# A gelu MLP with per-row experts in fp32r: block 1's first layer computed plainly, weight sums transposed on VectorE, x of block 0 loaded in two halves

## Chip, cores and metric

The kernel runs on one core of a Trainium2 chip. The metric is the device time of one execution in microseconds. One execution was also recorded by the hardware profiler; all rows shown here are from it.

## What is computed

```python
h = jax.nn.gelu(jnp.einsum('bnd,hd->bnh', x, fc1_w) + fc1_b, approximate=False)
shared = jnp.einsum('bnh,sh->bns', h, fc2_w) + fc2_b
We = experts_w[indices]
be = experts_b[indices]
expert_x = jnp.einsum('bnh,bph->bnp', h, We) + be[:, None, :]
x = x + jnp.concatenate([shared, expert_x], axis=-1)
```

x is 32 x 256 x 256, fc1_w 1024 x 256, fc2_w 192 x 1024; each of the 32 rows of the batch picks one of 16 experts of 64 x 1024. Everything is float32.

## The kernel before

Work goes in 16 blocks (n = 0 to 15) of two batch rows, so 512 tokens (4 tiles of 128). Each float32 operand is split in two fp32r parts, a high one (a copy, made by ScalarE) and a low one (the difference, made by VectorE or GpSimd), and each product is three matmuls: high by high, high by low, low by high. The engines run five hand-written instruction streams that meet only through semaphores, each in its written order.

**First layer (fc1).** Block 0 is computed plainly: `conv_chunk(j)` (j = 0 to 7) makes 128 hidden features for all 512 tokens with 6 matmuls of 512 columns, into one of four PSUM banks `fc1_ps`; ScalarE turns it into gelu, two chunks make a pair. Blocks 1 to 15 use a seven-product scheme on half-size matrices (`product`, L875): per block two groups, per group seven products of 6 matmuls of 256 columns, so 84 matmuls. It needs four sums of weight pieces (W_S1 to W_S4), made once, and four sums of x pieces per block (X_T1 to X_T4: `x_sum`, `x_sums_high`, `x_sums_lo`), and VectorE's adds (`add_c11`, `add_v`, `add_c12`, `add_c22`).

**Hidden features.** ScalarE's `pair_high` writes a pair's high part to `ht`, GpSimd's `pair_lo` (L303) the low part. ScalarE's `gelu_free` keeps it from overwriting a `gelu` buffer (there are two) until the low part of the pair that lay in it is done.

**Second layer (fc2).** `fc2_units(n, r, first, count)` multiplies pair r by the weights, 3 matmuls of 256 columns a unit (L911, L913, L915), 96 in all for a block. It runs one block behind fc1, its units put between the products. It writes `acc_ps`, one bank per batch row, which VectorE's `drain(n, b)` (L728) adds to `resid`. Before the first unit of block n on a bank TensorE waits for `drained` of block n - 1 on it:

```python
if r == 0 and n >= 1 and u in (0, T * 2):
    pe.wait_ge(drained, R * (n - 1) + b + 1)
```

**Start.** TensorE transposes block 0's x (`x0_bank`) and the fc1 weights (`w1_bank`), the latter by halves; between them it runs 20 and 10 small matmuls (`warm`) that compute nothing. The transposed weight sums also come from TensorE (`s_bank`, 16 transposes of 128x128 into `acc_ps`, from what GpSimd's `weight_sum` made of the rows of fc1_w). fc2_w, the experts and x of the later blocks come to `pieces` in 32-row pieces and are transposed by VectorE (`w2_square`, `experts_square`, `x_square`), through the two PSUM banks `tr_ps`. SyncE issues most loads (`load_x`, `load_w1`, `load_experts`, `load_x_pieces`), ScalarE's queue the first half of fc1_w, fc1_b and the expert numbers `index`. GpSimd's `residual(n)` (L295) adds the biases to `resid`.

In the trace's rows `fc_ps` is `fc1_ps`, and `work` holds fc1_w's rows and later scratch.

Of the kernel before, what the change touches and what calls it, by code (L numbers as in the profile page):

```python
# [15 lines left out]
def cond_mlp_residual(nc, x, index, fc1_w, fc1_b, fc2_w, fc2_b, experts_w, experts_b, out):  # L16
# [24 lines left out]
    X_B11, X_B21, X_B22, X_T1, X_T2, X_T3, X_T4 = range(7)  # L41
    BANK_A, BANK_B, BANK_C = (0, 1), 2, 3
# [12 lines left out]
    w1_v = fc1_w.rearrange("(q k c) d -> q c k d", q=Q, c=S)  # L55
    w2_v = fc2_w.rearrange("(a r) (q j) -> q r a j", r=S, q=Q)

    ctx = ExitStack()
    with ctx:
# [34 lines left out]
        s_in = work[:, 2048:4096].rearrange("p (s m c) -> p s m c", s=4, m=4)  # L94
# [18 lines left out]
        w1_loaded = [sem(f"w1_loaded{n}") for n in range(2)]  # L113
        w2_loaded = sem("w2_loaded")
# [11 lines left out]
        s_tr = sem("s_tr")  # L126
# [11 lines left out]
        x0_hi = sem("x0_hi")  # L138
        w1_hi = sem("w1_hi")
# [37 lines left out]
        def group(n, g):  # L177

            return GROUPS * (n - 1) + g

# [18 lines left out]
        def _(sp):  # L199
# [35 lines left out]
            load_x(0)  # L235
            load_w1(sp, 1)
            for q in range(Q):
# [8 lines left out]
                .then_inc(b2_loaded, 16)  # L246
            load_x(1)
# [41 lines left out]
        def _(pool):  # L289
            def residual(n):  # L290
                par = n % 2
                pool.wait_ge(x_loaded[par], 16 * (n // 2 + 1))
# [16 lines left out]
            def x_sums_lo(n):  # L309
                pool.wait_ge(xt_hi, n)  # L310
# [5 lines left out]
            def weight_rows(part, d):  # L316

                rows = w1_in.rearrange("p (h l j) (c d) -> p l d h j c", h=2, l=2, d=D)
                return rows[:, part, d]

            def weight_sum(s, in0, in1, op):
                nc.gpsimd.tensor_tensor(
                    s_in[:, s, :, :].rearrange("p (h j) c -> p h j c", h=2), in0, in1, op)\
                    .then_inc(s_added, 1)

            def made(s):
                return s_in[:, s, :, :].rearrange("p (h j) c -> p h j c", h=2)
# [7 lines left out]
            for half in range(2):  # L335
                pool.wait_ge(w1_loaded[half], 16 * Q)
# [6 lines left out]

            for r in range(PAIRS):
                pair_lo(r)
            x_sums_lo(1)
# [4 lines left out]
            for n in range(1, BLOCKS):  # L351
                for g in range(GROUPS):
                    t = group(n, g)
                    if t > 0:
                        pair_lo(PAIRS + 2 * (t - 1))
                        pair_lo(PAIRS + 2 * (t - 1) + 1)
# [4 lines left out]
            pair_lo(PAIRS + 2 * LAST_T)  # L361
            pair_lo(PAIRS + 2 * LAST_T + 1)

        @block.scalar
        def _(act):
# [17 lines left out]
            def s_high(s):  # L383
                act.wait_ge(s_tr, s + 1)
                if s == 3:

                    act.wait_ge(conv_filled, K)
                nc.scalar.activation(w1t[:, W_S1 + s, HI, :], acc_ps[:, s % 2, :], ACT.Copy)\
                    .then_inc(s_hi, 1)

            def w2_high(f):
# [3 lines left out]
                    tr_ps[:, f % 2, 0:2 * SHARED].rearrange("p (k c) -> p k c", k=2),  # L395
# [37 lines left out]
            def s1_copy(t):  # L433
# [3 lines left out]
                else:  # L437
                    act.wait_ge(w1_tr, 2 * D)
# [9 lines left out]
            def x_sums_high(n):  # L448
                act.wait_ge(t_added, 4 * n)
# [15 lines left out]
            def conv_chunk(j):  # L465
                act.wait_ge(conv_filled, j + 1)
                if j % 2 == 0:
                    gelu_free(j // 2)
                nc.scalar.activation(gelu[:, j // 2 % 2, j % 2, :], fc1_ps[:, j % 4, :],
                                     ACT.Gelu, bias=b1[:, j:j + 1]).then_inc(conv_gelu, 1)  # L470

            def conv_high(r):
                act.wait_ge(conv_gelu, 2 * r + 2)
                pair_high(r)

            def upper_pair(t):

                q = PAIRS + 2 * t
# [27 lines left out]

            load_w1(act, 0)
# [3 lines left out]
            act.dma_start(index_sb[:, :], index.rearrange("(o n) -> o n", o=1))\  # L511
                .then_inc(index_loaded, 16)
# [25 lines left out]
            conv_chunk(6)
            conv_chunk(7)
            conv_high(3)  # L540
            for half in range(2):
                experts_high(0, half)
            x_high(1)
            s_high(0)
            s_high(1)
            s_high(2)
            s_high(3)
            b_copy(1)
            x_sums_high(1)

            for n in range(1, BLOCKS):
# [20 lines left out]
        def _(dve):  # L572
# [18 lines left out]

            def s_low(s):
                dve.wait_ge(s_hi, s + 1)
                nc.vector.tensor_tensor(w1t[:, W_S1 + s, LO, :], acc_ps[:, s % 2, :],
# [3 lines left out]
            def w2_square(f):  # L598
                if f < 2:
                    dve.wait_ge(w2_loaded, 16 * Q)  # L600
                    dve.wait_ge(w1_lo, D + f + 1)
                else:
# [3 lines left out]
                    tr_ps[:, f % 2, 0:2 * SHARED].rearrange("p (k a c) -> p a k c", k=2, c=S),  # L606
# [3 lines left out]
            def w2_low(f):  # L610
# [4 lines left out]
                    tr_ps[:, f % 2, 0:2 * SHARED].rearrange("p (k c) -> p k c", k=2),  # L615
# [33 lines left out]

            def x_sums_first(n):  # L650

                if n > 1:
                    dve.wait_ge(xt_lo, n - 1)
                else:

                    dve.wait_ge(s_tr, 4)
                dve.wait_ge(b_copied, n)
                x_sum(0, b_rows[:, SEQ:2 * SEQ], b_rows[:, 0:SEQ])

                dve.wait_ge(xb_hi, 2 * n)  # L660
# [32 lines left out]
            def add_v(t):  # L693
# [5 lines left out]
                n = t // GROUPS + 1  # L699

                dve.wait_ge(t_added, 4 * min(n + 1, LAST) - 2)
                dve.wait_ge(xb_lo, 2 * min(n + 1, LAST) - 1)
# [44 lines left out]
            dve.wait_ge(w2_lo, 4)  # L747
# [274 lines left out]
```

## Time and profile before

| | |
|---|---|
| median of 3 runs | 380.73 us (380.22 to 380.85) |
| time of the profiled execution | 380.61 us |
| span inside it | 378.8 us |
| TensorE matmul busy | 361.0 us (95%), 2915 matmuls |
| ScalarE busy | 248.5 us (66%) |
| GpSimd busy | 232.8 us (61%) |
| VectorE busy | 211.8 us (56%) |

The 1.8 us between the span and the execution's time lie before the first and behind the last recorded instruction. TensorE is busy in all but about 18 us, so what matters is where these lie, and at which clock it runs.

### The profile page before, as it was taken

The numbers are of one execution on the slowest core, as the hardware profiler recorded it, in microseconds if no ns is written. First come the engines' busy times: TensorE is split into PE (matmuls) and PEld (weight loads), VectorE is DVE, ScalarE is ACT, GpSimd is POOL, SyncE is SP. The second block draws the span as 40 slices with busy tenths as digits, with TensorE's granted clock in tenths as the row PEclk, the third lists the DMA queues.
The fourth block names the chain that finished last, engine by engine and source line by source line (L and its number), as shares of the span: only waits on it lengthen the run. The fifth ranks groups of instructions, "written<-read, shape, count | busy, mean of one in ns | idle before, by whom it ended". The sixth has DMA issues, their size and how long they took to land.

```text
span 378.8 us, 7987 instructions
## 1 busy us (share of the span) xinstructions
PE 361.0 (95%) x2915; PEld 355.7 (94%) x2915; DVE 211.8 (56%) x357; ACT 248.5 (66%) x420; POOL 232.8 (61%) x105
## 2 busy tenths in 40 slices
PE   6952999999999999999999999999999999999996
PEld 5842999999999999999999999999999999999996
DVE  1477447567473747667373756757384756733331
ACT  2674357687675767777575768767576777755560
POOL 0780537766666777666667776666667766666490
PEclk9995799999999999999999999999999999999999
DMA  8769860616152250616244151626235032303011
GB/s 197 166 140 257 251 135 32 163 40 173 57 146 85 82 130 26 173 54 157 76 110 122 44 154 35 173 58 158 73 91 127 24 115 50 119 2 111 2 56 57
DMA packets 70433, 39.98 MB, mean 106 GB/s; under 512 B 39418, under 2 KB 70394, under 8 KB 70394
## 3 DMA queue, kind: packets, MB, share of 16 engines
q1 hardware_dynamic: 69776, 38.95, 39.0%
q10 hardware_dynamic: 618, 0.53, 0.7%
q8 instruction: 23, 0.38, 0.4%
q14 instruction: 16, 0.13, 0.1%
HBM read 27.92 MB, written 8.39 MB: 96 GB/s over the span
## 4 chain that ended last, share of the span: by engine, by line
PE 86%; issue 2%; POOL 1%; ACT 0%; DVE 0%; POOLq 0%
PE fc_ps L875 39%; PE acc_ps L911 16%; PE acc_ps L915 16%; PE acc_ps L913 16%; POOL ht L303 1%; ACT ht L460 0%; ACT gelu L483 0%; DVE work L710 0%; DVE resid L728 0%; POOLq L293 0%
## 5 line engine op out<-in xcount | busy, mean ns | idle before, releaser
L303 POOL TENSOR_TENSOR ht<-gelu,ht 128x1024 fp32r<-128x1024 f32 x64 | 154.8, 2419 | 115.2 <-ACT ht L460 115.2
L875 PE MATMUL fc_ps<-xt,w1t 128*128 128x256 f32 x1260 | 186.7, 284 | 3.8 <-DVE xt L678 3.8
L875 PEld LDWEIGHTS fc_ps<-xt,w1t 128*128 128x128 f32 x1260 | 167.5, 193 | 4.2 <-DVE xt L678 4.2
L911 PE MATMUL acc_ps<-w2t,ht 128*128 128x256 f32 x512 | 145.5, 284 | 0.1
L913 PE MATMUL acc_ps<-w2t,ht 128*128 128x256 f32 x512 | 145.4, 284 | 0.0
L915 PE MATMUL acc_ps<-w2t,ht 128*128 128x256 f32 x512 | 145.4, 284 | 0.0
L911 PEld LDWEIGHTS acc_ps<-w2t,ht 128*128 128x128 f32 x512 | 98.9, 193 | 0.3 <-POOL ht L303 0.3
L915 PEld LDWEIGHTS acc_ps<-w2t,ht 128*128 128x128 f32 x512 | 98.8, 193 | 0.0
L913 PEld LDWEIGHTS acc_ps<-w2t,ht 128*128 128x128 f32 x512 | 98.8, 193 | 0.0
L446 ACT ACTIVATE work<-fc_ps 128x512 f32<-128x512 f32 x30 | 17.9, 597 | 87.7 <-PE fc_ps L875 87.7
L460 ACT ACTIVATE ht<-gelu 128x1024 fp32r<-128x1024 f32 x64 | 67.8, 1059 | 3.5
L690 DVE TENSOR_TENSOR work<-fc_ps,work 128x512 f32<-128x512 f32 x30 | 20.7, 691 | 66.6 <-issue 62.5
L311 POOL TENSOR_TENSOR xt<-work,xt 128x1024 fp32r<-128x1024 f32 x15 | 36.0, 2397 | 12.5 <-ACT xt L450 12.5
L483 ACT ACTIVATE gelu<-work,b 128x512 f32<-128x512 f32 x60 | 39.8, 714 | 1.7 <-DVE work L710 1.7
L703 DVE TENSOR_TENSOR work<-fc_ps,work 128x512 f32<-128x512 f32 x30 | 20.8, 692 | 34.5 <-PE fc_ps L875 34.4
L295 POOL TENSOR_TENSOR resid<-resid,bias 128x1024 f32<-128x1024 f32 x16 | 38.6, 2412 | 0.0
L710 DVE TENSOR_TENSOR work<-fc_ps,work 128x512 f32<-128x512 f32 x30 | 20.8, 693 | 22.4 <-PE fc_ps L875 22.4
L728 DVE TENSOR_TENSOR resid<-acc_ps,resid 128x512 f32<-128x512 f32 x32 | 21.8, 682 | 10.8 <-PE acc_ps L915 10.8
L495 ACT ACTIVATE gelu<-work,b 128x256 f32<-128x256 f32 x60 | 27.0, 500 | 0.0
L718 DVE TENSOR_TENSOR work<-fc_ps,work 128x512 f32<-128x512 f32 x30 | 20.7, 688 | 8.3 <-PE fc_ps L875 8.3
L500 ACT ACTIVATE gelu<-fc_ps,b 128x256 f32<-128x256 f32 x60 | 24.9, 469 | 0.2 <-PE fc_ps L875 0.2
L632 DVE TENSOR_TENSOR w2t<-tr_ps,w2t 128x512 fp32r<-128x512 f32 x32 | 20.6, 687 | 3.1 <-ACT w2t L402 3.1
(49 smaller groups left out, 236.5 us busy)
## 6 DMA issues: line engine op xcount, KB each, us to landing
resid<-in_x SPq DMA_DIRECT2D x16, 512.0 KB, 4.0
pieces<-in_L_cond_experts_w SPq DMA_DIRECT2D x128, 64.0 KB, 2.0
out<-resid SPq DMA_DIRECT2D x32, 256.0 KB, 3.2
pieces<-in_x SPq DMA_DIRECT2D x60, 128.0 KB, 3.6
w2t<-w2t SPq DMA_DIRECT2D x4, 768.0 KB, 8.0
bias<-in_L_cond_experts_b SPq DMA_DIRECT2D x32, 32.0 KB, 2.8
pieces<-in_L_cond_fc_w SPq DMA_DIRECT2D x4, 192.0 KB, 7.8
work<-in_L_cond_fc_w ACTq DMA_DIRECT2D x4, 128.0 KB, 5.8
```

The costliest lines, as they stand in the source:

```text
L295: nc.gpsimd.tensor_tensor(rows, rows, bias[:, par, :, :].unsqueeze(2).to_broadcast([P, R, T, OUT]), ALU.add).then_inc(resid_ready, 1)
L303: nc.gpsimd.tensor_tensor(ht[:, slot, LO, :, :].rearrange("p k t -> p (k t)"), gelu[:, q % 2, :, :].rearrange("p k t -> p (k t)"), ht[:, s ...
L311: nc.gpsimd.tensor_tensor(xt[:, n % 2, X_T1:X_T4 + 1, LO, :], t_sum, xt[:, n % 2, X_T1:X_T4 + 1, HI, :].bitcast(FP32), ALU.subtract).then_ ...
L460: nc.scalar.activation(ht[:, q % PAIRS, HI, :, :].rearrange("p k t -> p (k t)"), gelu[:, q % 2, :, :].rearrange("p k t -> p (k t)"), ACT.C ...
L483: nc.scalar.activation(gelu[:, q % 2, j, :], upper[:, j, :], ACT.Gelu, bias=b1[:, k:k + 1]).then_inc(up_gelu, 1)
L495: nc.scalar.activation(gelu[:, q % 2, j, SEQ:2 * SEQ], c22[:, j, :], ACT.Gelu, bias=b1[:, k:k + 1]).then_inc(c22_gelu, 1)
L500: nc.scalar.activation(gelu[:, q % 2, j, 0:SEQ], fc1_ps[:, BANK_A[t % 2], j * SEQ:(j + 1) * SEQ], ACT.Gelu, bias=b1[:, k:k + 1]).then_inc( ...
L728: nc.vector.tensor_tensor(dst, acc_ps[:, b, :].rearrange("p (t o) -> p t o", t=T), dst, ALU.add).then_inc(drained, 1)
L875: last = nc.tensor.matmul(fc1_ps[:, dst, j * SEQ:(j + 1) * SEQ], w1t[:, w, wv, ms], xt[:, n % 2, o, xv, :], start=(fresh and j == 0 and at ...
L911: nc.tensor.matmul(dst, h_hi_t, w_hi, start=(r == 0 and u % (2 * T) == 0), stop=True, skip_group_check=True)
L913: nc.tensor.matmul(dst, h_hi_t, w_lo, start=False, stop=True, skip_group_check=True)
L915: last = nc.tensor.matmul(dst, h_lo_t, w_hi, start=False, stop=True, skip_group_check=True)
```

## The change

Blocks 0 and 1 are now both plain (`PLAIN = 2`); the seven-product scheme starts at block 2. TensorE alternates 4 units (12 matmuls) of block 0's second layer with one chunk of block 1's first. The low halves of block 1's four pairs are made by VectorE (`plain_low`) instead of GpSimd. The weight sums are made from fc1_w in 32-row pieces, loaded a second time (`load_w1_pieces`), and transposed by VectorE (`s_square`) into `tr_ps`; TensorE's `s_bank` is gone. fc2_w's transposes go through `acc_ps` in place of `tr_ps`. GpSimd makes the low halves of block 0's pairs 0 and 1 ahead of the weight sums. x of block 0 is loaded in two halves; SyncE waits for the first before it issues anything else. The expert numbers are now the first load of ScalarE's queue.

```diff
+    PLAIN = 2
+    PAIR_ORDER = (1, 3, 0, 2)
+    S_ORDER = (0, 2, 1, 3)
...
@@ block.sync
+            def load_w1_pieces():
+                for q in range(Q):
+                    sp.dma_start(w1_piece[S * q:S * (q + 1), :, :, :]
+                                 .rearrange("p q k j -> p (q k) j"), w1_pieces[q])\
+                        .then_inc(w1p_loaded, 16)
-            load_x(0)
+            for b in range(R):
+                ts = slice(b * T, (b + 1) * T)
+                sp.dma_start(resid[:, 0, ts, :], x_blocks[0][:, ts, :]).then_inc(x0_loaded[b], 16)
+            sp.wait_ge(x0_loaded[0], 16)
             load_w1(sp, 1)
...
+            sp.wait_ge(w1_tr, 2 * D)
+            load_w1_pieces()
             load_x(1)
@@ block.gpsimd
+            pair_lo(0)
+            pair_lo(1)
+            pool.wait_ge(w1p_loaded, 16 * Q)
             weight_sum(0, weight_rows(1, 0), weight_rows(1, 1), ALU.add)
...
-            for r in range(PAIRS):
-                pair_lo(r)
-            x_sums_lo(1)
+            pair_lo(2)
+            pair_lo(3)
...
             residual(0)
+            x_sums_lo(PLAIN)
+            residual(1)
@@ block.scalar
+            conv_chunk(12)
+            conv_chunk(13)
+            conv_high(6)
+            b_copy(PLAIN)
+            x_high(PLAIN)
+            conv_chunk(14)
+            x_sums_high(PLAIN)
             for half in range(2):
+                experts_high(1, half)
+            conv_chunk(15)
+            conv_high(7)
@@ block.vector
+            def s_square(s):
+                dve.wait_ge(s_added, S_ORDER.index(s) + 1)
+                nc.vector.transpose(
+                    tr_ps[:, S_ORDER.index(s) % 2, :].rearrange("p (i q c) -> p i q c", i=HALF, c=S),
+                    s_in[:, s].rearrange("p q i c -> p i q c")).then_inc(s_sq, 1)
+            def plain_low(q):
+                dve.wait_ge(h_hi, q + 1)
+                nc.vector.tensor_tensor(
+                    ht[:, q % PAIRS, LO, :, :].rearrange("p k t -> p (k t)"),
+                    gelu[:, q % 2, :, :].rearrange("p k t -> p (k t)"),
+                    ht[:, q % PAIRS, HI, :, :].rearrange("p k t -> p (k t)").bitcast(FP32),
+                    ALU.subtract).then_inc(plain_lo, 1)
@@ block.tensor
-            s_bank(0)
             conv_chunk(5)
-            s_bank(1)
             conv_chunk(6)
             conv_chunk(7)
-            s_bank(2)
-            s_bank(3)
-            for n in range(1, BLOCKS):
+            for at, (r, first) in enumerate(((0, 0), (1, 0), (0, 4), (1, 4),
+                                             (2, 0), (2, 4), (3, 0), (3, 4))):
+                fc2_units(0, r, first, 4)
+                if at == 0:
+                    pe.wait_ge(x1_lo, D)
+                conv_chunk(K + at)
+            for n in range(PLAIN, BLOCKS):
```

TensorE before, from the last plain chunk of block 0 to the first units of the second layer (each row is an instruction or a run of equal ones; in brackets the semaphores it waits for):

```order
L851 MATMUL fc_ps<-xt,w1t 128x512 [waits conv_gelu]
L851 MATMUL fc_ps<-xt,w1t 128x512 x5
L811 MATMUL acc_ps<-ident,work 128x128 [waits s_lo,s_added]
L811 MATMUL acc_ps<-ident,work 128x128 x3
L811 MATMUL acc_ps<-ident,work 128x128 [waits s_lo,s_added]
L811 MATMUL acc_ps<-ident,work 128x128 x3
L875 MATMUL fc_ps<-xt,w1t 128x256 [waits conv_gelu,xb_lo]
L875 MATMUL fc_ps<-xt,w1t 128x256 x5
L911 MATMUL acc_ps<-w2t,ht 128x256 [waits s_lo,w2_row,e_lo,h_lo]
```

Behind chunk 7 stood the last two weight-sum transposes and then a product of block 1 that waits for all of its x; they are gone.

TensorE now, at the end of the plain part: block 1's last chunk, block 2's first product, and block 1's first unit of the second layer:

```order
L967 MATMUL fc_ps<-xt,w1t 128x512 [waits conv_gelu]
L967 MATMUL fc_ps<-xt,w1t 128x512 x5
L991 MATMUL fc_ps<-xt,w1t 128x256 [waits conv_gelu,xb_lo]
L991 MATMUL fc_ps<-xt,w1t 128x256 x5
L1029 MATMUL acc_ps<-w2t,ht 128x256 [waits w2_copied,drained,e_lo,plain_lo]
```

The unit's wait for `drained` is the one quoted above, now met with only one product between it and block 0's last unit.

VectorE now, from block 1's third low half to the drains of block 0 (L728 in other rows: x_sum, L733: plain_low, L705 and L713: experts of block 1, L823: drain):

```order
L733 TENSOR_TENSOR ht<-gelu,ht 128x1024 [waits h_hi]
L728 TENSOR_TENSOR work<-work 128x256 [waits b_copied,s_sq]
L728 TENSOR_TENSOR work<-tr_ps,work 128x256 [waits xb_hi]
L768 TENSOR_TENSOR xt<-work,xt 128x256 [waits xb_hi]
L728 TENSOR_TENSOR work<-tr_ps,work 128x256 [waits t_added] x2
L773 TENSOR_TENSOR xt<-tr_ps,xt 128x2x256 [waits xb_hi]
L705 STREAM_TRANSPOSE tr_ps<-pieces 128x4x4x32 [waits e_loaded1,t_added,xb_lo]
L705 STREAM_TRANSPOSE tr_ps<-pieces 128x4x4x32
L713 TENSOR_TENSOR w2t<-tr_ps,w2t 128x2x4x64 [waits e_hi] x2
L733 TENSOR_TENSOR ht<-gelu,ht 128x1024 [waits h_hi]
L823 TENSOR_TENSOR resid<-acc_ps,resid 128x512 [waits resid_ready,acc_filled]
```

The drain of block 0's first bank stands behind all of block 2's x, block 1's experts and block 1's last low half.

## Rows read from the trace of the kernel before

**Rows 1.** Stretches of the start: busy time of each engine, granted clock, DMA share.

```profile
24.00:28.60 4.60, 0.00 (x0) 0.00 (x0) 4.57 (x7) 2.72 (x4) 3.85 (x2) 1.00 0.86 216
28.60:37.10 8.50, 1.94 (x8) 1.57 (x8) 5.80 (x12) 4.26 (x8) 0.43 (x1) 0.50 0.96 253
37.10:42.25 5.15, 5.15 (x24) 5.15 (x25) 1.32 (x2) 2.29 (x5) 4.63 (x2) 0.50 1.06 323
42.25:60.25 18.00, 18.00 (x152) 18.00 (x152) 10.12 (x18) 10.03 (x16) 7.01 (x4) 1.00 0.53 126
60.25:376.00 315.75, 315.10 (x2625) 314.72 (x2623) 181.26 (x305) 215.69 (x366) 205.12 (x87) 1.00 0.34 91
```

**Rows 2.** TensorE's timeline: start, length, what, count, idle before.

```profile
1.53 3.89 PE L817 MATMUL fc_ps<-ident 128*128 128x256 bf16 x20 [1.53 <-POOL ident L331]
5.86 1.23 PE L811 MATMUL tr_ps<-ident,resid 128*128 128x128 f32 x8 [0.44 <-DMA resid<-in_x]
6.92 1.25 PE L817 MATMUL fc_ps<-ident 128*128 128x256 bf16 x10
9.29 1.22 PE L811 MATMUL acc_ps<-ident,work 128*128 128x128 f32 x8 [1.11 <-DMA work<-in_L_cond_fc_w]
10.72 1.83 PE L858 MATMUL fc_ps<-xt,w1t 128*128 128x512 f32 x6
13.25 5.73 PE L851 MATMUL fc_ps<-xt,w1t 128*128 128x512 f32 x24
...
31.36 1.94 PE L811 MATMUL acc_ps<-ident,work 128*128 128x128 f32 x8 [7.37 <-DVE w1t L594]
37.10 1.65 PE L875 MATMUL fc_ps<-xt,w1t 128*128 128x256 f32 x6 [3.80 <-DVE xt L678]
...
60.33 0.88 PE L875 MATMUL fc_ps<-xt,w1t 128*128 128x256 f32 x6
```

**Rows 3.** ScalarE's timeline, same columns: gelu of a chunk, high half of a pair.

```profile
15.98 1.06 ACT L460 ACTIVATE ht<-gelu 128x1024 fp32r<-128x1024 f32 x1
16.93 0.69 ACT L469 ACTIVATE gelu<-fc_ps,b 128x512 f32<-128x512 f32 x1
...
25.72 1.07 ACT L402 ACTIVATE w2t<-tr_ps 128x512 fp32r<-128x512 f32 x2
```

**Rows 4.** GpSimd's timeline, same columns.

```profile
10.09 5.16 POOL L322 TENSOR_TENSOR work<-work 128x512 f32<-128x512 f32 x4 [8.62 <-DMA work<-in_L_cond_fc_w]
17.12 2.40 POOL L303 TENSOR_TENSOR ht<-gelu,ht 128x1024 fp32r<-128x1024 f32 x1 [1.87 <-ACT ht L460]
...
62.86 2.40 POOL L303 TENSOR_TENSOR ht<-gelu,ht 128x1024 fp32r<-128x1024 f32 x1
```

**Rows 5.** VectorE's timeline, same columns.

```profile
24.91 1.91 DVE L751 CAST w2t<-w2t 128x1536 fp32r<-128x1536 f32 x2
26.74 1.27 DVE L632 TENSOR_TENSOR w2t<-tr_ps,w2t 128x512 fp32r<-128x512 f32 x2
28.05 1.32 DVE L643 STREAM_TRANSPOSE tr_ps<-pieces 128x512 f32<-128x512 f32 x2
...
34.58 0.42 DVE L647 TENSOR_TENSOR work<-work 128x256 f32<-128x256 f32 x1
...
36.37 0.68 DVE L678 TENSOR_TENSOR xt<-tr_ps,xt 128x512 fp32r<-128x512 f32 x1
...
59.76 0.68 DVE L728 TENSOR_TENSOR resid<-acc_ps,resid 128x512 f32<-128x512 f32 x1
...
64.80 0.75 DVE L647 TENSOR_TENSOR work<-work 128x256 f32<-128x256 f32 x1
```

**Rows 6.** DMA issues of SyncE's and ScalarE's queues: count, KB each, median us to landing.

```profile
pieces<-in_x SPq DMA_DIRECT2D x60, 128.0 KB, 3.6
out<-resid SPq DMA_DIRECT2D x32, 256.0 KB, 3.2
work<-in_L_cond_fc_w SPq DMA_DIRECT2D x4, 128.0 KB, 6.1
```

**Rows 7.** SyncE's timeline: start and length of its issues of the experts of block 0.

```profile
10.59 3.83 SPq L209 DMA_DIRECT2D pieces<-in_L_cond_experts_w  x8
```

More of the change, by code:

```diff
@@ L291, in residual @@
                 par = n % 2
-                pool.wait_ge(x_loaded[par], 16 * (n // 2 + 1))
+                if n == 0:
+                    for b in range(R):
+                        pool.wait_ge(x0_loaded[b], 16)
+                else:
+                    pool.wait_ge(x_loaded[par], 16 * ((n + 1) // 2))
                 pool.wait_ge(be_loaded[par], 16 * R * (n // 2 + 1))
@@ L736, in _ @@
             nc.vector.tensor_copy(b1[:, :], fc1_ps[:, 3, 0:K]).then_inc(b1_ready, 1)
-            for d in range(D):
-                w1_low(1, d)
             w2_square(0)
             w2_square(1)
+            w1_low(1, 0)
             w2_low(0)
             w2_square(2)
+            w1_low(1, 1)
             w2_low(1)
@@ L757, in _ @@
                 x_square(1, d)
-            for s in range(4):
-                s_low(s)
-            x_sums_first(1)
-            x_low(1, 0)
-            x_sums_last(1)
-            x_low(1, 1)
-            for n in range(1, BLOCKS):
+            for d in range(D):
+                x1_low(d)
+            dve.wait_ge(w2_lo, 4)
+            for cols in (slice(0, SHARED), slice(OUT, OUT + SHARED)):
+                nc.vector.tensor_copy(w2t[:, 0, 1, :, cols], w2t[:, 0, 0, :, cols].bitcast(FP32))\
+                    .then_inc(w2_row, 1)
+            dve.wait_ge(x1_lo, D)
+            s_square(0)
+            s_square(2)
+            plain_low(4)
+            s_low(0)
+            s_low(2)
+            dve.wait_ge(s_lo, 2)
+            s_square(1)
+            s_square(3)
+            plain_low(5)
+            s_low(1)
+            s_low(3)
+            dve.wait_ge(s_lo, 4)
+            for d in range(D):
+                x_square(PLAIN, d)
+            plain_low(6)
+            x_sums_first(PLAIN)
+            x_low(PLAIN, 0)
+            x_sums_last(PLAIN)
+            x_low(PLAIN, 1)
+            dve.wait_ge(xb_lo, 2)
+            dve.wait_ge(t_added, 4)
+            for half in range(2):
+                experts_square(1, half)
+            for half in range(2):
+                experts_low(1, half)
+            plain_low(7)
+            drain(0, 0)
+            for n in range(PLAIN, BLOCKS):
                 for g in range(GROUPS):
@@ L818, in warm, with x0_banks @@
                                      start=True, stop=True)
-            def x0_bank(d):
-                transposes(tr_ps[:, d, :], [feature_chunk(resid[:, 0, t, :], d)
-                                            for t in range(TILES)]).then_inc(x0_tr, 1)
+            def x0_banks(b):
+                pe.wait_ge(x0_loaded[b], 16)
+                for d in range(D):
+                    last = transposes(tr_ps[:, d, b * SEQ:(b + 1) * SEQ],
+                                      [feature_chunk(resid[:, 0, b * T + t, :], d)
+                                       for t in range(T)])
+                    if b == R - 1:
+                        last.then_inc(x0_tr, 1)
             def w1_bank(half, d):
@@ L923, in _ @@
             warm(WARM)
-            pe.wait_ge(x_loaded[0], 16)
-            for d in range(D):
-                x0_bank(d)
+            for b in range(R):
+                x0_banks(b)
             warm(WARM // 2)
```

240 lines of the change are left out of this document (133 added, 107 removed).

## The prediction

> **What bounds the kernel now.** I read the stretches first [rows 1]. From 42.25 us on TensorE has no gap to speak of until 376 us, at a granted clock of 1.00 (its 2.4 GHz level): 152 matmuls in 18.00 us, 0.12 us each, are its rate for 256 columns, and 2625 matmuls in 315.75 us say the same. So only the start can give time. There TensorE does nothing from 24.00 to 28.60, and 8 matmuls from 28.60 to 37.10 at clock 0.50 (1.2 GHz). Its timeline [rows 2] names the waits: 7.37 us until the low half of a weight sum came and the next transposes could go (31.36), and 3.80 us until block 1's x sums were done (37.10). Then 24 matmuls run at 0.50 for 5.15 us [rows 1]; at 0.12 us they would take 2.88. So in front of block 1's products lie 11.2 us of idleness, 1.94 us of transposes and 2.3 us lost to the clock. Block 2's first product starts at 60.33 [rows 2]. That is my mark, for from there on both kernels do the same, but for one product of block 1 (6 matmuls, 0.72 us) that before stood behind it and is now gone.
>
> **The first microseconds.** The two x halves cannot help before 5.4 us, where the 20 warming matmuls end (1.53 + 3.89, [rows 2]); before, x let them wait until 5.86. Eight transposes (1.06 to the next instruction) and ten warming matmuls (1.1) bring TensorE to 7.5 us. There it needs the first half of fc1_w, which came at 9.29 with x, the other half and fc2_w in flight. Now only x and that half (1 MB) are, since SyncE's queue is held until x's first half has landed. 256 KB lands in 3.2 us elsewhere [rows 6]; a half issued until 2.8 us is there between 6.0 us (as fast as that) and 9.3 us (no gain). I take "by 7.5", so the transposes move 1.8 us up. Behind the waiting SyncE stand the second half and fc2_w: issued from about 4.2 us on, with 6.1 us to landing at worst [rows 6] the last of the half is there at some 10 to 12 us, while TensorE wants it at 10.6; I take no wait. The experts of block 0, issued at 10.59 [rows 7], now need not wait for late expert numbers and go at about 8.3. The second load of fc1_w, 1 MB in 256-byte runs, is issued at about 16 to 18 us; its wait for the transposes (11.7 us) is over by then. The x pieces, of such runs, take 3.6 us for 128 KB with three like them in flight [rows 6], so 1 MB is there at 21.5 to 25.
>
> **Up to block 1's first chunk.** Chunk 1 starts at 11.5 (13.25 less 1.8). Chunks cost 1.4 us (24 matmuls in 5.73, [rows 2]). The first pair's high half, before at 15.98 [rows 3], has a fc2 copy and a gelu in front of it now and starts at 15.2. The low half on GpSimd (2.40, [rows 4]) ends at 18.7, and chunk 4's gelu waits for it, as chunk 6's does for the second (22.9). TensorE waits 1.0 us for the last low weights ahead of chunk 4 (VectorE now puts fc2_w's squares before them) and ends chunk 7 at 22.3. On VectorE the experts' low halves are done at 24.2 (their highs on ScalarE come in 1.07 us [rows 3], lows in 1.27, [rows 5]), the transposes of x in 1.32 more and their high and low halves at 27.0. So TensorE idles 1.95 us, does 12 matmuls, idles 1.3 us and starts chunk 8 at 27.0. That replaces the wait of 24.00 to 37.10.
>
> **The plain block.** 8 chunks at 1.40 and 7 groups of 12 matmuls at 0.12 are 21.3 us: chunk 15 ends at 48.3. In columns alone the plain block costs TensorE 48 x 0.233 = 11.2 us where the scheme costs 84 x 0.12 = 10.1; 1.1 us more, less the 0.7 us of weight-sum transposes that stood between chunks. What else lies under it: the weight sums (5.16 on GpSimd, rows 4, to 28.5), the low halves of pairs 2 and 3 (to 33.5). TensorE wants pair 2 at 36.9, so 5 us of slack cover a late second fc1_w. The casts on VectorE (1.91, [rows 5]) and the sums' transposes, priced as x's, fit between. They cost nothing, since TensorE needs of ScalarE and VectorE there only the gelu of the chunk four back, which is ready 5 us ahead (chunk 8's at 31.7, chunk 12 starts at 38.4).
>
> **The wait that comes in its place.** Block 2's first product goes at 48.45 (its x's low half is due at 48.4, below), and 0.72 us later TensorE stands before `drained`. I follow that drain back from chunk 13, whose matmuls end at 42.9. ScalarE: gelu 43.5, high half (1.06) 44.65. VectorE: `plain_low(6)`. No row shows this operation, two SBUF inputs of 1024 columns. From below: 256 columns take 0.42 us [rows 5], 512 take 0.68 to 0.69, so 1.05 ns a column, which gives 1.23. From above: with GpSimd at work the 256-column one with two SBUF inputs takes 0.75 instead of 0.42 (64.80 and 34.58, [rows 5]; GpSimd's 2.40 from 62.86, [rows 4]), 0.33 more, so four times that is 1.3 more, 2.55. Here GpSimd is idle: 1.23, to 45.9. Then block 2's x sums and low halves, 34.58 to 37.05 before [rows 5], 2.5: 48.4. Experts of block 1: first transpose 49.15, highs on ScalarE 50.35, then, only now, chunk 15's gelu 50.95 and pair 7's high half 52.1. `plain_low(7)`: GpSimd has done the x sums' low part (48.9 to 51.3) and is in `residual(1)` to 53.7, so between 53.3 and 54.7; I take 54.2. Drain 0.68 [rows 5]: TensorE goes on at 55.0. It has then been idle for 5.8 us. Queued behind the waiting unit on TensorE are all further products, so nothing covers it.
>
> Of the Trainium skill, the page "SBUF — State Buffer", section "SBUF: two separate sides", bears on this: VectorE with two SBUF inputs and GpSimd exclude each other, and the later one is blocked for the whole instruction. By that rule `plain_low(7)` starts at 53.7 and TensorE goes on at 55.6. The 0.75 us rows fit the rule within 0.13 us (65.26 plus 0.42 is 65.68, the row ends at 65.55), so they do not decide between the two.
>
> **The sum.** Before, the unit behind block 2's first product stood at 61.05; now at 55.0: -6.05. The product gone behind it: -0.72. So -6.8, and 373.8 us if the clock stays up. But it fell 4.6 us after TensorE's last matmul (24.00 to 28.60) and came back 5.15 us after it was busy again, which cost 2.3 us [rows 1]. The stall of 5.8 is longer than 4.6, so I take the clock as falling at about 53.9: +2.4. Sum: -4.4, against the profiled execution's 380.61, which is 0.1 below the median of 380.73: **376.2 us**. Behind it I cost everything at nothing: the products, units and adds stand in the order of before, where TensorE waited for none of them, and the x pieces and experts that blocks 2 and 3 need are issued by 45 and 54 us.
>
> **Rivals.** (1) The clock stays up through the stall: 373.8. For it: only one fall is on record, at 4.6 us, and the stall may be a little shorter than I have it. (2) The stall is about 1.5 us shorter, because `plain_low(7)` is not slowed and ScalarE's handovers are quicker, with no fall of the clock: 372.4. (3) Full blocking between VectorE and GpSimd, as worked out above, by the order of what holds SBUF at 52.1 us: 376.8. (4) The change does not do what it says at the loads: the first half of fc1_w comes no earlier than 9.29, since the DMA engines are as full as before; everything up to chunk 8 moves back by 1.7: 377.9. (5) On the other side: the clock falls in the gaps between 22.3 and 27.0 us (3.25 us idle in 4.7, the longest stretch 1.95, against 4.6 at the fall on record) and stays at 0.50 through the plain block, whose groups wait on each other. The 21.3 us of it then take 42.6, the stall is the same, and the time is 395. It decides from 13.6 us of low clock on (6.8 gained divided by one half). Against it: 5.15 us of unbroken work brought the clock back, and the plain block has no wait in it.
>
> **Chances.** Forecast 0.48; (1) 0.22; (2) 0.08; (3) 0.08; (4) 0.09; (5) 0.02; the rest, 0.03, for a wait I have not seen. The range goes from 372.4 (2) to 378.4 (4, with the second half of fc1_w 0.5 late too). Within 0.2% (0.8 us) is what a measurement of this kernel cannot tell from no change: from 380.0 to 381.5. Faster 0.92, same 0.03, slower 0.05.
>
> **What the changed kernel's profile would show.** Transposes of fc1_w at 7.5 us, not 9.3 (loads). Chunk 8 at 27 us. No TensorE wait in the 21 us after it. `plain_low` at 1.2 us alone and 2 or more beside GpSimd. One TensorE wait of 5 to 6.5 us, released by VectorE's drain, right behind the first product of block 2, and clock 0.50 from near its end for some 5 us. I am wrong if that wait is under 3 us, if chunk 8 starts later than 29, or if TensorE waits for GpSimd's low halves between the plain chunks.

## The result

The changed kernel takes 382.42 us (median of 11 runs, 380.8 to 383.77), the kernel before 380.55 us beside it (11 runs). The ratio is 1.0054 (95% interval 1.0042 to 1.0066). So it is half a per cent slower. I had forecast 376.2.

The page of the changed kernel, its span and busy times, then the 40 slices of TensorE and of its clock:

```profile
span 380.6 us, 7848 instructions
...
PE 362.1 (95%) x2863; PEld 354.1 (93%) x2863; DVE 215.6 (57%) x353; ACT 244.5 (64%) x410; POOL 220.0 (58%) x100
...
PE   8978875999999999999999999999999999999996
...
PEclk9999696999999999999999999999999999999999
```

The long hole of before is gone, and the clock is low twice instead of once. Stretches of the changed kernel that answer to [rows 1], cut where its waits lie:

```profile
34.00:36.30 2.30, 2.30 (x15) 1.82 (x13) 0.73 (x1) 0.00 (x0) 2.22 (x3) 1.00 0.73 176
36.30:39.24 2.94, 0.12 (x2) 0.00 (x1) 0.00 (x0) 0.00 (x0) 2.94 (x3) 0.88 0.61 153
39.24:45.30 6.06, 6.06 (x22) 5.48 (x23) 3.63 (x2) 5.51 (x8) 4.62 (x2) 0.50 1.05 330
45.30:53.30 8.00, 8.00 (x52) 7.11 (x50) 7.93 (x14) 5.36 (x9) 0.00 (x0) 0.99 0.80 225
53.30:55.60 2.30, 1.15 (x8) 0.76 (x6) 2.23 (x5) 1.23 (x2) 0.40 (x1) 1.00 0.65 146
55.60:61.69 6.09, 0.05 (x1) 0.03 (x1) 5.05 (x6) 3.14 (x5) 4.26 (x2) 0.78 0.68 156
61.69:66.00 4.31, 4.31 (x21) 4.31 (x21) 1.70 (x4) 1.36 (x3) 0.00 (x0) 0.52 0.59 180
66.00:376.00 310.00, 309.91 (x2583) 309.74 (x2582) 177.42 (x299) 210.48 (x356) 197.77 (x83) 1.00 0.33 90
```

From 66 us on nothing waits, as before. TensorE's timeline, to set beside [rows 2]:

```profile
7.17 1.12 PE L930 MATMUL acc_ps<-ident,work 128*128 128x128 f32 x8
...
26.31 1.65 PE L967 MATMUL fc_ps<-xt,w1t 128*128 128x512 f32 x6 [1.00 <-DVE xt L741]
...
34.88 1.55 PE L967 MATMUL fc_ps<-xt,w1t 128*128 128x512 f32 x6
39.24 0.58 PE L1029 MATMUL acc_ps<-w2t,ht 128*128 128x256 f32 x1 [2.82 <-POOL ht L353]
...
54.69 0.97 PE L991 MATMUL fc_ps<-xt,w1t 128*128 128x256 f32 x6 [1.16 <-DVE xt L773]
61.69 0.55 PE L1029 MATMUL acc_ps<-w2t,ht 128*128 128x256 f32 x1 [6.04 <-DVE resid L823]
```

fc1_w's transposes start at 7.17 and chunk 8 at 26.31: the forecast had 7.5 and 27.0. The last row is the stall behind block 2's first product, 6.04 us and released by the drain: forecast 5.8. What was not forecast stands between. TensorE waits until 39.24 for a low half from GpSimd, inside the plain block; it waits again, 1.16 us, for block 2's x sums, ahead of that block's first product; and the unit behind the stall goes at 61.69, not 55.0. Backwards from there, SyncE's queue, then GpSimd, then ScalarE:

```profile
16.04 0.43 SPq L287 DMA_DIRECT2D bias<-in_L_cond_fc_b  x1
16.52 9.71 SPq L271 DMA_DIRECT2D work<-in_L_cond_fc_w  x4
26.27 1.98 SPq L255 DMA_DIRECT2D resid<-in_x  x1
```

```profile
31.71 5.18 POOL L375 TENSOR_TENSOR work<-work 128x512 f32<-128x512 f32 x4 [9.25 <-DMA work<-in_L_cond_fc_w]
36.85 4.68 POOL L353 TENSOR_TENSOR ht<-gelu,ht 128x1024 fp32r<-128x1024 f32 x2
41.48 2.38 POOL L346 TENSOR_TENSOR resid<-resid,bias 128x1024 f32<-128x1024 f32 x1
...
57.52 2.34 POOL L346 TENSOR_TENSOR resid<-resid,bias 128x1024 f32<-128x1024 f32 x1
```

```profile
39.28 1.27 ACT L527 ACTIVATE gelu<-fc_ps,b 128x512 f32<-128x512 f32 x2 [12.08 <-POOL ht L353]
```

The four issues of the second load of fc1_w took 9.71 us, not 2; it had landed at about 31.7 us, where I had 21.5 to 25. GpSimd sat idle for it 9.25 us with pairs 2 and 3 of block 0 behind the sums in its order, and ScalarE 12.08 us for the buffer that pair 2 lay in. The same load, the shortest, median and longest of its four issues (in ns) and of their landings (in us):

```profile
L271 SPq DMA_DIRECT2D work<-in_L_cond_fc_w x4: 503/825/7427, 16.5 to 25.1; - x4
...
DMA to landing us min/median/max: 6.5/10.1/11.3
```

One issue alone took 7.43 us.

### The profile page after: what moved, and what is told of

The parts are those of the page before. It is cut to its first block, busy times and chain, and to the rows that moved or that the text cites. A ratio compares the mean times of both kernels' runs of the same rounds, so it can differ in the third digit from the quotient of the medians.

```text
span 380.6 us, 7848 instructions
## 1 busy us (share of the span) xinstructions
PE 362.1 (95%) x2863; PEld 354.1 (93%) x2863; DVE 215.6 (57%) x353; ACT 244.5 (64%) x410; POOL 220.0 (58%) x100
## 4 chain that ended last, share of the span: by engine, by line
PE 79%; SPq 5%; issue 5%; DVE 3%; POOL 3%; DMA 2%; ACT 2%; DVEq 0%; POOLq 0%; ACTq 0%
PE fc_ps L991 36%; PE acc_ps L1029 15%; PE acc_ps L1033 15%; PE acc_ps L1031 15%; SPq L271 2%; POOL ht L353 2%; DMA work<-in_L_cond_fc_w 2%; POOL work L375 1%; ACT ht L515 1%; SPq L243 1%; DMA resid<-in_x 1%; DVE w1t L675 1%; SPq L260 0%; DVE ht L733 0%; SPq L282 0%
## 5 line engine op out<-in xcount | busy, mean ns | idle before, releaser
L353 POOL TENSOR_TENSOR ht<-gelu,ht 128x1024 fp32r<-128x1024 f32 x60 | 144.4, 2408 | 120.6 <-ACT ht L515 120.6
L991 PE MATMUL fc_ps<-xt,w1t 128*128 128x256 f32 x1176 | 173.7, 284 | 1.2 <-DVE xt L773 1.2
L991 PEld LDWEIGHTS fc_ps<-xt,w1t 128*128 128x128 f32 x1176 | 155.8, 193 | 1.6 <-DVE xt L773 1.6
L785 DVE TENSOR_TENSOR work<-fc_ps,work 128x512 f32<-128x512 f32 x28 | 19.4, 692 | 60.6 <-issue 58.0
L361 POOL TENSOR_TENSOR xt<-work,xt 128x1024 fp32r<-128x1024 f32 x14 | 33.6, 2402 | 21.1 <-ACT xt L505 21.1
L346 POOL TENSOR_TENSOR resid<-resid,bias 128x1024 f32<-128x1024 f32 x16 | 38.5, 2406 | 0.0
L541 ACT ACTIVATE gelu<-work,b 128x512 f32<-128x512 f32 x56 | 37.2, 715 | 1.8 <-DVE work L805 1.8
L798 DVE TENSOR_TENSOR work<-fc_ps,work 128x512 f32<-128x512 f32 x28 | 19.3, 691 | 32.5 <-PE fc_ps L991 32.3
L805 DVE TENSOR_TENSOR work<-fc_ps,work 128x512 f32<-128x512 f32 x28 | 19.4, 692 | 21.0 <-PE fc_ps L991 21.0
L823 DVE TENSOR_TENSOR resid<-acc_ps,resid 128x512 f32<-128x512 f32 x32 | 21.7, 679 | 10.8 <-PE acc_ps L1033 10.8
L967 PE MATMUL fc_ps<-xt,w1t 128*128 128x512 f32 x90 | 23.8, 411 | 1.8 <-DVE xt L741 1.0
L553 ACT ACTIVATE gelu<-work,b 128x256 f32<-128x256 f32 x56 | 25.2, 500 | 0.0
L813 DVE TENSOR_TENSOR work<-fc_ps,work 128x512 f32<-128x512 f32 x28 | 19.2, 686 | 7.8 <-PE fc_ps L991 7.8
L558 ACT ACTIVATE gelu<-fc_ps,b 128x256 f32<-128x256 f32 x56 | 23.3, 469 | 0.2 <-PE fc_ps L991 0.2
```

The source lines that it names most:

```text
L346: nc.gpsimd.tensor_tensor(rows, rows, bias[:, par, :, :].unsqueeze(2).to_broadcast([P, R, T, OUT]), ALU.add).then_inc(resid_ready, 1)
L353: nc.gpsimd.tensor_tensor(ht[:, slot, LO, :, :].rearrange("p k t -> p (k t)"), gelu[:, q % 2, :, :].rearrange("p k t -> p (k t)"), ht[:, s ...
L361: nc.gpsimd.tensor_tensor(xt[:, n % 2, X_T1:X_T4 + 1, LO, :], t_sum, xt[:, n % 2, X_T1:X_T4 + 1, HI, :].bitcast(FP32), ALU.subtract).then_ ...
L541: nc.scalar.activation(gelu[:, q % 2, j, :], upper[:, j, :], ACT.Gelu, bias=b1[:, k:k + 1]).then_inc(up_gelu, 1)
L553: nc.scalar.activation(gelu[:, q % 2, j, SEQ:2 * SEQ], c22[:, j, :], ACT.Gelu, bias=b1[:, k:k + 1]).then_inc(c22_gelu, 1)
L558: nc.scalar.activation(gelu[:, q % 2, j, 0:SEQ], fc1_ps[:, BANK_A[t % 2], j * SEQ:(j + 1) * SEQ], ACT.Gelu, bias=b1[:, k:k + 1]).then_inc( ...
```

## Experiments

All times are medians; ratios are against the kernel before, timed on the same chip, where it took 380.3 to 380.55 us. Four theories were tested. Two are of the late load: A, that the broadcast of fc2_b ahead of it in the queue holds it up; B, that its own 256-byte runs are slow. Theory C says that the order on GpSimd turns the lateness into time, and theory D that TensorE's 6 us stall comes from where the drain stands.

### e1_bias_last: the broadcast behind the load

```diff
+            sp.wait_ge(w1_tr, 2 * D)
+            load_w1_pieces()
+            load_x(1)
             sp.dma_start(
                 bias[:, :, :, 0:SHARED].rearrange("p a b o -> p (a b) o"),
...
-            sp.wait_ge(w1_tr, 2 * D)
-            load_w1_pieces()
-            load_x(1)
```

> The fc2_b broadcast load is issued behind the second load of fc1_w and x of block 1 instead of ahead of them; nothing else changes. Theory A (the broadcast of 512 packets of 768 bytes trickles from 17.5 to 24 us and holds up what is queued behind it): the four issues of the second fc1_w load take about 2 us instead of 9.7, it lands at about 22 us, GpSimd's weight sums start at about 23 instead of 31.7, TensorE has no wait in the plain block, its wait for the drain ends at about 55 instead of 61.7, and the time is 375 to 377 us. Theory B (the load is slow by its own 4096 runs of 256 bytes): issues still 8 to 10 us, sums at 29 to 32, time 381 to 383.

378.18 us, ratio 0.9948 (0.9928 to 0.9969). SyncE's issue and GpSimd's sums:

```profile
15.87 4.84 SPq L271 DMA_DIRECT2D work<-in_L_cond_fc_w  x4
```

```profile
26.62 6.60 POOL L374 TENSOR_TENSOR work<-work 128x512 f32<-128x512 f32 x4 [2.98 <-DMA work<-in_L_cond_fc_w]
```

Neither expectation was met in full. From the first issue to the sums it is 10.75 us in place of 15.19, so the broadcast cost 4.4 of them, but the load is not as quick as A had it. TensorE's wait inside the plain block is gone, yet it waits longer for block 2's x sums, 2.23 us for 1.16, and the time stays above A's 375 to 377:

```profile
51.14 1.47 PE L990 MATMUL fc_ps<-xt,w1t 128*128 128x256 f32 x6 [2.23 <-DVE xt L772]
```

### e9_rows_1k and e10_rows_1k_bias_last: longer runs

The second load brings the same bytes in runs of 1 KB, in the first load's layout, so the weight sums are of wrong pieces; e10 also has the broadcast behind.

```diff
-                    sp.dma_start(w1_piece[S * q:S * (q + 1), :, :, :]
-                                 .rearrange("p q k j -> p (q k) j"), w1_pieces[q])\
+                    sp.dma_start(w1_in[S * q:S * (q + 1), :, :], w1_v[q])\
```

> The changed kernel, its second load of fc1_w taken in runs of 1 KB in the layout of the first (so the weight sums are of wrong pieces), same bytes, same place in SyncE's order, the fc2_b broadcast still ahead of it. With 256-byte runs the four issues took 9.7 us and the sums started 15.2 us after the first of them; with the broadcast behind, 4.8 and 10.7 us. If the broadcast and the runs each cost their own part, this one lies between: sums start 8 to 11 us after the first issue, time 378 to 380. If the run length is nothing, it is as the changed kernel, 382.4.

> e9_rows_1k with the fc2_b broadcast behind the load as in e1_bias_last. Both causes gone: issues take about 2 us, sums start 5 to 7 us after the first issue, at about 23, as in the kernel without this load; time 376.5 to 377.5. If the load is slow for a third reason (experts' biases, full queue), sums start at 26 or later.

381.99 us (1.0039, 1.0025 to 1.0053) and 378.16 us (0.9946, 0.9924 to 0.9967): what the runs of 256 bytes took in the same places. SyncE and GpSimd of e9, then of e10:

```profile
16.59 6.84 SPq L271 DMA_DIRECT2D work<-in_L_cond_fc_w  x4
```

```profile
30.87 5.18 POOL L374 TENSOR_TENSOR work<-work 128x512 f32<-128x512 f32 x4 [8.37 <-DMA work<-in_L_cond_fc_w]
```

```profile
16.16 1.91 SPq L271 DMA_DIRECT2D work<-in_L_cond_fc_w  x4
```

```profile
25.95 6.49 POOL L373 TENSOR_TENSOR work<-work 128x512 f32<-128x512 f32 x4 [2.50 <-DMA work<-in_L_cond_fc_w]
```

The four kernels make a square. From first issue to sums: 15.2 (256 bytes, broadcast ahead), 14.3 (1 KB, ahead), 10.75 (256 bytes, behind), 9.8 (1 KB, behind). The broadcast ahead costs 4.4 and 4.5 us, the short runs 0.9 and 0.95. Two other kernels with this load as in the changed one, e2 and e4 below, give 14.9 and 14.1, so the 0.9 is not clear of the spread, while the 4.4 is. A is right about most of what can be had, B about little. Both e9 and e10 missed what was expected of them, 8 to 11 us to the sums and sums at about 23. The 9.8 us that are left for 1 MB, with experts and x in flight around it, are still more than I gave it, and no run takes them apart: that part of the cause stays open.

### e2_low_first: pairs 2 and 3 ahead of the weight sums

```diff
             pair_lo(0)
             pair_lo(1)
+            pair_lo(2)
+            pair_lo(3)
             pool.wait_ge(w1p_loaded, 16 * Q)
...
-            pair_lo(2)
-            pair_lo(3)
```

> GpSimd makes the low halves of block 0's pairs 2 and 3 ahead of the weight sums; the loads stay as they are. If the late sums hurt only because these two low halves stood behind them (ScalarE's 12 us wait, TensorE's 2.8 us wait, the fall of the clock at 39 us), the wait for the drain now ends at 54 to 56 us and the time is 375 to 377. If the sums themselves are needed that early (their high and low halves stand in VectorE's and ScalarE's order ahead of block 2's x), it ends later: sums are done at about 37 us where the forecast had 28, and the time is 378 to 380.

376.65 us, ratio 0.9908 (0.9893 to 0.9923). C holds: the sums come as late as in the changed kernel (31.45), and 5.8 us of 382.42 are gone with two calls moved. TensorE and VectorE at the stall:

```profile
48.72 0.98 PE L991 MATMUL fc_ps<-xt,w1t 128*128 128x256 f32 x6
55.73 0.55 PE L1029 MATMUL acc_ps<-w2t,ht 128*128 128x256 f32 x1 [6.02 <-DVE resid L823]
```

```profile
52.35 2.63 DVE L733 TENSOR_TENSOR ht<-gelu,ht 128x1024 fp32r<-128x1024 f32 x1 [0.97 <-ACT ht L515]
```

The forecast had 48.45 for the first of them, and for the second 55.0, or 55.6 if VectorE is fully blocked.

### e3_no_second_load: the load taken out

The sums are taken from the first load's rows in the wrong layout.

```diff
-            load_w1_pieces()
...
-            pool.wait_ge(w1p_loaded, 16 * Q)
+            pool.wait_ge(w1_loaded[0], 16 * Q)
+            pool.wait_ge(w1_loaded[1], 16 * Q)
```

> Leaves out the second load of fc1_w: the weight sums are taken from the first load's rows, in the wrong layout, and GpSimd waits for that load instead. It prices the load as a whole. If the lateness of this load is all that the forecast missed: sums start right behind pair 1's low half at 22.5 us, wait for the drain ends at about 54.5, time 374.5 to 376.5. If something else in the plain block is late too (VectorE's low halves beside GpSimd, the gelu handovers), it stays at 378 or more.

376.86 us, ratio 0.9905 (0.989 to 0.992), 0.4 above what I expected at most. GpSimd, then TensorE:

```profile
23.73 5.88 POOL L374 TENSOR_TENSOR work<-work 128x512 f32<-128x512 f32 x4
```

```profile
55.93 0.56 PE L1029 MATMUL acc_ps<-w2t,ht 128*128 128x256 f32 x1 [6.04 <-DVE resid L823]
```

With the load gone altogether the kernel is no faster than with the two low halves moved. So the load's lateness cost 5.6 us, all of it, within the noise, by the order on GpSimd.

### e4_no_hold and e7_loads_only: what holding SyncE does

e4 takes the wait out of the changed kernel. e7 puts the three edits of the loads alone (x in two loads, SyncE's wait, expert numbers first) into the kernel before.

```diff
-            sp.wait_ge(x0_loaded[0], 16)
             load_w1(sp, 1)
```

> SyncE no longer waits for the first half of x before it issues its other loads; x stays in two loads. TensorE's transposes of fc1_w then start at about 9.3 us as in the kernel before, 2.1 us later than now. If the start lies on the path to the end, the time is 384 to 384.5. If the path runs through SyncE's queue and the late second load, whose issue comes 1 to 1.5 us earlier without the wait, the time is 381 to 382, no slower.

> The kernel before with one part of the change alone: x of block 0 in two loads, SyncE held until the first has landed, expert numbers first in ScalarE's queue. TensorE's transposes of fc1_w then start 0.7 to 2 us earlier than 9.29. The path from there to 37.1 us runs over ScalarE's and VectorE's chain of block 0, which starts as much earlier, so the time should fall by 1 to 2 us, to 378.5 to 379.5; if the chain is held by the later landing of fc2_w or of the experts, it stays at 380.4.

e4: 380.57 us, ratio 1.0007 (0.9995 to 1.0018). e7: 378.0 us, ratio 0.9941 (0.9927 to 0.9954). Both are 0.4 to 0.5 us below what was expected at best. TensorE and GpSimd of e4, then TensorE of e7:

```profile
8.60 1.12 PE L929 MATMUL acc_ps<-ident,work 128*128 128x128 f32 x8
...
52.70 1.65 PE L990 MATMUL fc_ps<-xt,w1t 128*128 128x256 f32 x6 [3.56 <-DVE xt L772]
```

```profile
29.61 5.18 POOL L374 TENSOR_TENSOR work<-work 128x512 f32<-128x512 f32 x4 [5.72 <-DMA work<-in_L_cond_fc_w]
```

```profile
7.72 1.12 PE L819 MATMUL acc_ps<-ident,work 128*128 128x128 f32 x8
...
35.43 1.65 PE L888 MATMUL fc_ps<-xt,w1t 128*128 128x256 f32 x6 [3.80 <-DVE xt L686]
```

In e7 the transposes start 1.57 us ahead of [rows 2] and block 1's first product 1.67 ahead, and the time falls by 2.3. In the changed kernel the same wait loses: without it the kernel is 1.85 us faster. There the path ran through SyncE's queue to the late load, which came 2.1 us earlier, and block 2's first product went 2.0 us earlier with it (52.70), though TensorE had started its transposes 1.4 us later. How much of the start's gain is the hold's own stays open, since the 20 warming matmuls ahead of the transposes took 3.7 to 3.8 us in some profiles and 4.4 to 4.5 in others. Among the latter the transposes start at 8.60 us without the hold (e4) and at 7.84 to 8.49 with it (e1 to e3, e5, e8, e10, e11).

### e5_early_drains and e6_drains_bias_last: the drain moved

On top of e2; e6 has the broadcast behind as well.

```diff
                 x_square(PLAIN, d)
+            drain(0, 0)
             plain_low(6)
...
                 experts_low(1, half)
+            drain(0, 1)
             plain_low(7)
-            drain(0, 0)
```

> On top of e2_low_first, VectorE drains block 0's first bank ahead of the third low half of block 1 and its second bank ahead of the fourth, instead of both behind the fourth. If TensorE's 6.0 us stall behind block 2's first product is the price of where the drain stands, it shrinks to the 2 to 3 us until block 1's experts are ready (51.5 us in place of 55.7), the clock stays at 1.00, and the time is 369.5 to 371.5 (376.65 less 4 for the stall and 2.3 for the clock). If something else releases the unit just as late (experts, the fc2 copies by DMA), it stays above 374.

> e5_early_drains with the fc2_b broadcast also moved behind the second load of fc1_w and x of block 1. The weight sums start 4 to 5 us earlier (at 27). With the low halves of block 0 ahead of them nothing waits for the sums in e2_low_first, so the time should be that of e5_early_drains within 0.5 us. If the sums are still on the path there, this one is 1 us or more faster.

370.97 us (0.9772, 0.9753 to 0.9792) and 370.99 us (0.976, 0.9741 to 0.9779). e5, TensorE and a stretch with the clock:

```profile
51.61 0.36 PE L1031 MATMUL acc_ps<-w2t,ht 128*128 128x256 f32 x1 [1.78 <-DVE w2t L713]
```

```profile
50.00:55.00 5.00, 3.39 (x28) 3.42 (x29) 4.56 (x5) 2.90 (x5) 4.09 (x2) 1.00 0.75 168
```

D holds. The unit goes at 51.61 instead of 55.73, released by the experts' weights, the clock stays at 1.00, and 5.7 us are gone: 4.1 of stall, and 1.6 that I put down to the clock, as the difference. Once nothing waits for the sums, the broadcast's place is worth nothing that these medians show. (In e6 the sums start at 29.81 us, not at 27, since GpSimd is at the low halves until then.)

### e8_residual_later: GpSimd out of VectorE's way

On top of e2, `residual(1)` behind block 3's x sums.

```diff
             x_sums_lo(PLAIN)
-            residual(1)
...
                         x_sums_lo(n + 1)
+                    if t == 0:
+                        residual(1)
```

> On top of e2_low_first, GpSimd adds the biases to block 1's rows one operation later, behind the x sums of block 3 instead of behind those of block 2, so that it is idle while VectorE makes the fourth low half of block 1. If VectorE with two SBUF inputs is blocked until GpSimd's instruction ends (in the changed kernel 58.31 to 60.94, GpSimd's ending at 59.86), this low half takes 1.2 us instead of 2.63, the stall is 4.6 us instead of 6.0 and the time 375.2; and if the clock does not fall in the shorter stall, 373. If it is not GpSimd that stretches it, the time stays at 376.6.

374.9 us, ratio 0.9869 (0.9854 to 0.9885). VectorE, TensorE and two stretches:

```profile
52.10 1.23 DVE L734 TENSOR_TENSOR ht<-gelu,ht 128x1024 fp32r<-128x1024 f32 x1 [0.97 <-ACT ht L516]
```

```profile
54.07 0.55 PE L1030 MATMUL acc_ps<-w2t,ht 128*128 128x256 f32 x1 [4.63 <-DVE resid L824]
```

```profile
50.00:55.00 5.00, 0.93 (x4) 0.96 (x5) 4.02 (x6) 2.52 (x4) 1.35 (x1) 0.86 0.70 164
55.00:60.00 5.00, 5.00 (x37) 5.00 (x36) 2.95 (x8) 1.96 (x4) 0.00 (x0) 0.80 0.70 157
```

The low half takes 1.23 us instead of 2.63, and the stall 4.63 instead of 6.02. The clock still fell, at about 53.6, for 3.4 us.

### e11_all

e5 with the broadcast behind and `residual(1)` later.

> Low halves of block 0 first, early drains, fc2_b broadcast behind, and block 1's biases one operation later. In the runs with early drains TensorE no longer waits for the low half that GpSimd stretched, so the last edit should bring nothing there: 370.5 to 371.3, the same as e5_early_drains. If VectorE's stretched instruction still delayed TensorE behind it, 0.5 to 1 us less.

370.43 us, ratio 0.9745 (0.9727 to 0.9764), as expected: with the drains early TensorE does not wait for that low half. The medians of e11 and e5 differ by 0.5 us, so no worth of the last two edits is shown there.

## Why the prediction was wrong

**The first microseconds: right, in part by luck.** The transposes start at 7.17 us for 7.5. So they do in e6 and e9 (7.16 and 7.20), where the warming matmuls took 3.7 to 3.8 us too. In the seven other kernels that hold SyncE as the changed kernel does, they start at 7.84 to 8.49.

**The first step that failed: the second load of fc1_w.** I wrote that it is issued at about 16 to 18 us and "there at 21.5 to 25", priced by the x pieces, and that 5 us of slack cover it. It was there at 31.7. I took issues at 0.5 us each and did not look at what stands ahead in the queue. The broadcast of fc2_b has a row of its own in the list of DMA issues of the kernel before, 9.1 us to landing, the longest there. I used it nowhere. In the square of e1, e9 and e10 it costs 4.4 us, the short runs some 0.9, which is not clear of the spread, and the rest is a load that takes about 10 us and not 5.5 to 9.

**The second: the slack was 2 us, not 5.** The weight sums ran from 31.71 to 36.9, where I had 23.3 to 28.5, and so pair 2's low half, which stands behind them on GpSimd, ended at 39.2 instead of 31.0. I measured the slack only to TensorE's own use of pair 2, at 36.9, and wrote of the other engines' work under the plain block that it costs nothing. But chunk 8's gelu on ScalarE needs the buffer that pair 2 lies in, and behind that gelu VectorE's order runs from `plain_low` of pair 4 to block 2's x sums. In the changed kernel VectorE is busy without a gap from 41.67 us to their last low half, which ends at 54.63:

```profile
53.95 0.68 DVE L773 TENSOR_TENSOR xt<-tr_ps,xt 128x512 fp32r<-128x512 f32 x1
```

The same marks in every kernel that keeps the drains where they were, `residual(1)` in its place and block 1 plain, in us, with the time of the profiled execution:

| kernel | pair 2's low half ends | block 2's first product | unit behind the stall | time |
|---|---|---|---|---|
| changed | 39.20 | 54.69 | 61.69 | 382.42 |
| e9 | 38.42 | 53.97 | 60.98 | 382.06 |
| e4 | 37.15 | 52.70 | 59.70 | 381.18 |
| e1 | 35.58 | 51.14 | 58.15 | 378.55 |
| e10 | 34.81 | 50.36 | 57.37 | 377.96 |
| e3 | 32.69 | 48.91 | 55.93 | 377.46 |
| e2 | 27.69 | 48.72 | 55.73 | 376.91 |

In the first five the product goes 15.5 to 15.6 us behind pair 2's low half, released by VectorE each time, whatever TensorE did before it. (2.1 us of the 15.5 are `plain_low` of pair 4, held up by GpSimd's `residual(0)`, see below.) In e2 and e3 TensorE comes to the product without a wait. So for a product at 48.45 pair 2 had to be done by 32.9, 2 us behind my 31.0. It was 8.2 us late, and the product 6.2. I had a wait for GpSimd's low halves in the list of what would show me wrong, but gave it no price and no chance of its own.

**The clock, a second time, at no cost.** My rival 5 named gaps of the plain block as a danger and put them before chunk 8. The clock fell in the 2.8 us wait behind chunk 11 instead: 0.88 over 36.30 to 39.24 is 0.7 us at 0.50, so at about 38.5, 2.1 us after the last matmul (34.88 + 1.55). The 6.06 us at 0.50 held TensorE's chunks up by about 3.0 us. But chunk 15 ended at 53.4 and the x sums came at 54.63: with a quicker TensorE the product would have waited for VectorE so much longer. e4 had no wait and no low clock in the plain block, and stood 3.56 us at the product. e9 had the fall where rival 5 put it: the clock is at 0.50 from about 25.0 to 31.8 us. It cost nothing either, as TensorE still stood 3.78 us at the product:

```profile
26.35 2.93 PE L966 MATMUL fc_ps<-xt,w1t 128*128 128x512 f32 x6 [0.80 <-DVE xt L740]
...
53.97 1.65 PE L990 MATMUL fc_ps<-xt,w1t 128*128 128x256 f32 x6 [3.78 <-DVE xt L772]
```

"It fell 4.6 us after the last matmul" is what one row showed, and no constant.

**The sum of the miss.** Block 2's first product went at 54.69 instead of 48.45, 6.2 us late. From it to the unit behind the stall it is 7.0 us in all seven kernels where I had 6.55, so the unit stands at 61.69 instead of 55.0. From there on it is 320.7 us (382.42 less 61.69) where I had 321.2 (376.2 less 55.0), and 320.4 to 321.5 in the seven. That gives 382.42 instead of 376.2.

**The wait that came in its place: right.** 6.04 us for 5.8, by the drain, with a fall of the clock. With the load's lateness taken off the path (e2) the kernel is at 376.65, its product at 48.72 and its unit at 55.73. (On the way there I wrote 44.65 for 43.5 plus 1.06, which is 44.56; nothing hangs on it.)

**VectorE beside GpSimd: rival 3 was right.** I gave it 0.08. In e2 the unit goes at 55.73, where full blocking gives 55.6 and my own value was 55.0. The changed kernel's `plain_low` of pairs 4, 5 and 7:

```profile
41.67 3.27 DVE L733 TENSOR_TENSOR ht<-gelu,ht 128x1024 fp32r<-128x1024 f32 x1 [6.67 <-ACT ht L515]
...
47.40 1.20 DVE L733 TENSOR_TENSOR ht<-gelu,ht 128x1024 fp32r<-128x1024 f32 x1
...
58.31 2.63 DVE L733 TENSOR_TENSOR ht<-gelu,ht 128x1024 fp32r<-128x1024 f32 x1 [0.97 <-ACT ht L515]
```

Alone it takes 1.20 us (I had 1.23). The other two end at 44.94 and 60.94; GpSimd's `residual` ended at 43.86 (41.48 + 2.38) and 59.86 (57.52 + 2.34). Both end 1.08 us behind it, though they had started 0.2 and 0.8 us into it. Had VectorE run on at some share of its speed, the one with the longer overlap, 2.2 us for 1.6, would have had less left to do at the end of `residual`; a VectorE that is blocked until the other's end gives this. The Trainium skill says, in "SBUF — State Buffer", section "SBUF: two separate sides", that of two such instructions the one that starts first keeps the shared ports for its whole length and the other is blocked, and here the traces agree. It was worth 1.4 us of the stall (e8).

## What to carry to other kernels

A load that is added behind others in a queue can be held up by them: read the time to landing of each row of the issues. Here a broadcast with 9.1 us to landing cost the load behind it 4.4, and putting it behind took them away. Count the slack of a transfer along every chain that starts from it, through the other engines too, and not only to the next wait of the busiest engine; here that made 2 us of 5. When an operation depends on a new, uncertain transfer, look at what stands behind it in that engine's order and does not need it; moving two such calls was worth 5.8 us here. And where two phases meet, put the instruction that frees an accumulator ahead of work that only comes later; that was 5.7 us, and both together turn +0.5% into -2.3%.

## What the runs showed of the hardware

A broadcast of 768-byte rows to 128 partitions (384 KB) takes 9.3 us to land in the changed kernel, and delays what is issued behind it. The longest of the four issues of the next load took 7.43 us with the broadcast ahead and 256-byte runs, 3.14 with 1 KB runs (e9), 2.53 with 256-byte runs and the broadcast behind (e1), and 0.45 with neither (e10), so both lengthen it:

```profile
L271 SPq DMA_DIRECT2D work<-in_L_cond_fc_w x4: 432/450/451, 16.2 to 17.6; - x4
```

Casts are held up beside GpSimd too: the two `CAST`s of 1536 columns took 1.82 us in the changed kernel with GpSimd idle and 4.53 in e2 beside two of its low halves. The clock fell 4.6 us after the last matmul in the kernel before and 2.1 us after it in the changed one; in e9 it fell at about 25.0 us, with TensorE at work again since 23.68 behind an idle stretch of 1.79 us, while the changed kernel (1.71 us idle, at work from 23.64) and e1 (1.81 us idle) passed the same place at 1.00. The length of one gap does not tell whether it falls.
